# Later requests and later splits of the first second-layer weights in a mixture-of-experts kernel

## The reference

```python
hid  = jax.nn.relu(jnp.einsum('nd,edf->nef', h_flat, exp_w1) + exp_b1)   # D = 256 -> FF = 1024
eout = jnp.einsum('nef,efd->ned', hid, exp_w2) + exp_b2                  # FF = 1024 -> D = 256
y    = jnp.einsum('ned,ne->nd', eout, combine)                           # two experts a row
x    = x + y.reshape(x.shape)
...
df    = -gradv_Af + gradvv_Bf * 0.5
f_new = f + df * dt[:, None, None]
return jnp.maximum(f_new, 0.0)
```

## Time and profile before

| | |
|---|---|
| three executions | 357.04 us median (356.84, 357.04, 358.08) |
| the profiled execution's own time | 358.11 us |
| its span | 356.3 us |
| TensorE busy | 304.0 us, 85% of the span |
| VectorE busy | 285.2 us, 80% |
| ScalarE busy | 252.6 us, 71% |
| GpSimd busy | 160.7 us, 45% |
| DMA moved | 74.27 MB, mean 208 GB/s |

### The profile page before, as it was taken

One profiled execution on the slowest core, in us unless ns is written; L12 is line 12 of the kernel. 1 busy time (PEld: TensorE's weight loads), 2 busy tenths in 40 slices (PEclk: granted clock), 3 DMA queues, 4 the chain that ended last, 5 costly groups with the idle time before them and its releaser, 6 DMA issues.

```text
span 356.3 us, 6562 instructions
## 1 busy us (share of the span) xinstructions
PE 304.0 (85%) x1963; PEld 264.1 (74%) x1963; DVE 285.2 (80%) x523; ACT 252.6 (71%) x465; POOL 160.7 (45%) x136
## 2 busy tenths in 40 slices
PE   1759133899999999999999999999999988467886
PEld 0648123899999999999999999999999978122334
DVE  4896773598899889988888988998898893299991
ACT  1688213796997899699699979969978870188421
POOL 2566306144345445543533554554354413287650
PEclk9999655899999999999999999999999999699999
DMA  7904355886677787766867886776784500596832
GB/s 270 379 7 127 110 225 168 312 265 218 213 256 264 269 278 254 263 198 244 281 205 261 266 294 208 247 242 224 229 266 152 158 3 30 171 300 118 179 103 77
DMA packets 49860, 74.27 MB, mean 208 GB/s; under 512 B 3349, under 2 KB 40751, under 8 KB 49712
## 3 DMA queue, kind: packets, MB, share of 16 engines
q1 hardware_dynamic: 45104, 62.29, 53.5%
q0 software_dynamic: 4368, 11.54, 10.6%
q10 hardware_dynamic: 368, 0.20, 0.2%
HBM read 63.51 MB, written 9.31 MB: 204 GB/s over the span
## 4 chain that ended last, share of the span: by engine, by line
PE 72%; DVE 13%; DMA 6%; ACT 3%; issue 3%; POOL 1%; SPq 1%; DVEq 0%; POOLq 0%; ACTq 0%
PE psum L1005 24%; PE psum L1032 19%; PE psum L1034 10%; PE psum L998 5%; PE psum L974 2%; PE psum L1000 2%; PE psum L1027 2%; DMA t_y<-y_rows 2%; PE psum L1069 1%; DMA x_sb<-t_y 1%; PE psum L913 1%; PE psum L924 1%; DMA x_sb<-in_x_dram 1%; PE psum L1068 1%; DVE t_d1b2f L1540 1%
## 5 line engine op out<-in xcount | busy, mean ns | idle before, releaser
L798 POOL DMA_INDIRECT gathered<-h_rows,src_cur x40 | 64.9, 1622 | 123.1 <-DVE src_cur L1336 103.3
L1032 PE MATMUL psum<-w_split,hid 128*128 128x512 f32 x296 | 106.7, 403 | 1.4 <-DVE y_sb L1388 1.4
L1005 PE MATMUL psum<-slot_h,w_split 128*128 128x256 f32 x768 | 97.4, 287 | 2.3 <-DVE slot_h L1353 1.5
L1005 PEld LDWEIGHTS psum<-slot_h,w_split 128*128 128x128 f32 x768 | 95.4, 195 | 3.5 <-issue 2.9
L1034 PE MATMUL psum<-w_split,hid 128*128 128x256 f32 x296 | 82.8, 280 | 0.0
L1347 DVE TENSOR_TENSOR w_split<-raw_b,w_split 128x2048 fp32r<-128x2048 f32 x23 | 52.7, 2292 | 19.6 <-ACT w_split L622 19.6
L1032 PEld LDWEIGHTS psum<-w_split,hid 128*128 128x128 f32 x296 | 55.6, 188 | 14.1 <-issue 1.7
L654 ACT ACTIVATE hid<-relu 128x512 fp32r<-128x512 f32 (+1 forms) x92 | 51.0, 590 | 16.4 <-DVE relu L1359 16.4
L811 POOL DMA_INDIRECT y_rows<-y_sb,dst_cur x39 | 48.7, 1249 | 28.6 <-issue 11.6
L645 ACT ACTIVATE relu<-psum,b_cur 128x256 f32<-128x256 f32 x128 | 53.6, 490 | 10.8 <-PE psum L1005 9.0
L1341 DVE TENSOR_TENSOR w_split<-raw_a,w_split 128x2048 fp32r<-128x2048 f32 x23 | 52.6, 2285 | 8.8 <-DMA gathered<-h_rows,src_cur 5.9
(11 more groups left out here) (184 smaller groups left out, 395.3 us busy)
## 6 DMA issues: line engine op xcount, KB each, us to landing
raw_a<-in_L_cond_exp_w_dram SPq DMA_DIRECT2D x23, 1024.0 KB, 6.2
raw_b<-in_L_cond_exp_w_dram SPq DMA_DIRECT2D x23, 1024.0 KB, 5.6
t_y<-y_rows SPq DMA_DIRECT2D x6, 512.0 KB, 8.4
x_sb<-in_x_dram SPq DMA_DIRECT2D x4, 512.0 KB, 6.7
h_rows<-h_tok SPq DMA_DIRECT2D x16, 128.0 KB, 2.2
x_sb<-t_y POOLq DMA_DIRECT2D x4, 512.0 KB, 4.8
out_dram<-t_out SPq DMA_DIRECT2D x3, 512.0 KB, 3.0
b_all<-in_L_cond_exp_b_dram SPq DMA_DIRECT2D x1, 1024.0 KB, 10.4
```

Of the source, the lines that this page charges most:

```text
L798: pool.indirect_dma_start(out=gathered[:, par, t, :], out_offset=None, in_=h_rows, in_offset=bass.IndirectOffsetOnAxis(ap=src_cur[:, par, ...
L1005: last = pe.matmul(banks[bank][:, ST * (blk % 2):ST * (blk % 2) + rows], w_split[:, 0, par, w, at:at + P], slot_h[:, par, h, k, 0:rows], s ...
L1032: pe.matmul(out.rearrange("p (w d) -> p w d", w=2), hid[:, par, 0, blk, P * t:P * t + P], w_split[:, 1, par, :, D * blk:D * blk + D], star ...
```

## The change

The wait in front of the load of the second weights of slots 0 and 1 is now for slot 1's rows, where it was for slot 0's. On ACT, the high part of slot 0's second weights is made behind the fourth bank's relus, where it stood behind the first bank's high part, ahead of the high part of slot 1's rows. On DVE its low part is made behind the low part of the second bank, where it stood ahead of it.

```diff
-            sp.wait_ge(rows_in[0], moved(0, None))
+            sp.wait_ge(rows_in[1], moved(1, None))
             for s in range(2):
                 sp.dma_start(w2_raw[s].rearrange("p (b d) -> p b d", b=FB),
...
                 relus(k, m, 1)
                 high(k, m, 0)
                 if k == 0:
-                    split_w2(0, None)
                     split_h(1, None)
                 relus(k, m, 2)
                 high(k, m, 1)
                 relus(k, m, 3)
+                if k == 0:
+                    split_w2(0, None)
                 if k > 0 and not last_slot:
                     split_h(k + 1, m)
...
                     if k == 0:
                         low_h(1, None)
+                    low_hid(k, m, 1)
+                    if k == 0:
                         low_w2(0, None)
-                    low_hid(k, m, 1)
```

## The result

The changed kernel took 360.23 us in the median (359.06 to 360.94, 7 executions), the kernel before 358.08 us (356.84 to 358.42, 7 executions, the three of the prediction among them). The ratio is 1.0066 with a 95% interval of 1.0047 to 1.0085: slower by about 2.1 to 2.4 us, where no change that can be measured was forecast (+0.2 us, with 358.6 as the range's upper end). On the 357.04 us that the forecast started from, the ratio makes 359.4, outside the range as well. The profiled execution took 360.23 us, with a span of 358.4; the one of before had 358.11 and 356.3.

The account below looks back on a forecast made before the run. TensorE was taken to bound the kernel, with 1.14 us of waits to win and ACT and DVE close behind. The -0.76 us gain is given back in a new wait of about 1.0, leaving +0.2: median 357.3 us, range 356.3 to 358.6.

Parts of the forecast that it names:

- the chain through ACT and DVE: Through slot 0's finish to layer 2 of slot 1: ends at 85.20 before, 0.76 us ahead of TensorE; 86.17 after.
- the new wait: TensorE ahead of layer 2 of slot 1, released by DVE's finish of slot 0: about 1.0 us, giving back the -0.76.
- the load of slot 2's first weights: SP's third 1 MB load: lands at 73.2 instead of 69.46; ACT waits 0.4 us and is 0.97 us later than before.
- the upper bound: Slot 2's first weights land as much later as their group starts, 4.6 us, at 74.1.
- a lower bound with 422 GB/s for the third MB: Slot 2's first weights: two loads alone took 7.66 us, a third MB adds 2.5, landing at 72.25.
- the slots behind move with TensorE's +0.2: Behind slot 3's rows, ACT and DVE have idle time to fall back on, so later slots shift by only +0.2 us.
- executions with an early clock: TensorE's clock rises earlier in the ramp: the change loses up to 0.8 us more, +0.2 becoming +1.0.
- all cases with the load or the clock dearer: Rival, chance 0.25: load lands at 74.1 (+0.9) or clock rises early (+0.8), 357.7 to 358.6; both, +1.9 or 358.9.
- TensorE did not keep its gain: Rival, chance 0.16: TensorE keeps its gain at layer 2 of slot 1, up to -1.08 us, 356.0 to 356.6.
- The rows did come earlier: Rival, chance 0.05: slot 1's rows do not come earlier, SP's wait ends at 65.9; +4.9 us, 362.
- The clock did not fall: Rival, chance 0.02: TensorE's clock falls back in the new wait, products at half speed, 359 to 360.
- the signs of being wrong: TensorE has no new wait before layer 2 of slot 1, or ACT's split stands behind its DMA past 74.5.

Follow-up runs that it names:

- e3: Changed kernel, with SP's loads reordered: slot 0's second weights, slot 2's first weights, slot 1's second weights; ratio to the kernel before 1.0002.
- e5: e3, with DVE's finish of slot 0 put ahead of the low part of slot 1's second weights; 357.34 on 357.44 us, 0.9994.
- a1: Changed kernel, no edit, profiled again, clock nearly late; layer 2 of slot 1 starts 27.56 us after slot 0's first product.
- a2: Changed kernel, no edit, profiled again, early clock; layer 2 of slot 1 starts 27.31 us after slot 0's first product.
- e1: Kernel before, with only SP's wait moved to slot 1's rows and ACT's and DVE's order kept; 360.45 on 357.65 us, 1.0076.
- e4: Changed kernel, with slot 3's first weights asked for behind slot 2's second weights; ratio to the kernel before 1.0059.
- e6: Changed kernel, with DVE's index for slot 2's gather made behind the low part of slot 1's rows, so the gather issues later; 360.8 us, 1.0098.
- b1: Kernel before, no edit, profiled again, late clock; layer 2 of slot 1 starts 25.73 us after slot 0's first product.
- b2: Kernel before, no edit, profiled again, early clock; layer 2 of slot 1 starts 24.98 us after slot 0's first product.
- e2: Changed kernel, with SP's wait put back to slot 0's rows, only ACT's and DVE's order moved; 358.98 on 357.65 us, 1.0025.
- e7: Kernel before, with ACT's high part of slot 1's rows ahead of the split of slot 0's second weights; ratio 0.9998.
- e8: e7 plus e5's early finish; SP loads slot 0's second weights, then behind slot 1's rows slot 2's first and slot 1's second; 0.9997.

## Why the prediction was wrong

**What came as forecast.** Slot 1's rows land at 61.95 (62.1 was said), and their transposes follow the first half without a wait. Layer 1 of slot 1 follows at once. The moved split starts at 69.65 (69.88), its DMA in time. Layer 2 of slot 0 starts at 75.23 (75.4). ACT is ready for the split of slot 2's first weights at 72.7 (72.82). From there the chain through ACT and DVE to the finish of slot 0 and to layer 2 of slot 1 is the one named, and the new wait ends on L1389. e3 and e5 confirm its two ends: with the load in time the loss is gone, with the finish moved that wait is gone.

**The step that failed** is "the load of slot 2's first weights". The mechanism was right, the term was too small. I took 73.2 for its landing, the middle between 72.25 and 74.1; it was 74.44. ACT's wait was 1.83 us instead of 0.4, and its start 2.28 us later than before instead of 0.97. In distances from slot 0's first product the split comes 1.48 us later than was said (14.55 against 73.2 - 60.13 = 13.07), and layer 2 of slot 1 1.43 later than the +0.2: this one term is that part of the miss. The grounds for going below the upper bound were that slot 1's gathers no longer share the way, and a lower bound with 422 GB/s for the third MB. The group of three took 12.4 to 12.8 us in the six profiles in which it starts with slot 1's rows (after, a1, a2, e1, e4, e6), more than the 11.8 to 12.1 in the five with slot 1's gathers beside it (before, b1, b2, e2, e7). The nearest row was the group's own, and the upper bound made from it was itself 0.3 us too early.

The estimate by the Trainium skill, DMA: Bandwidth & Descriptors, section "Anatomy of one DMA" (71.3), was 3.1 us too early. The section gives its fit for DMAs issued by GpSimd, and these loads are issued by SP; the prediction did not say so. By the prediction's own sum a load in time would also have lowered the result by 0.4 us (ACT at 72.82 instead of 73.2), not by 0.2.

**The second miss** is in the sum's end: "the slots behind move with TensorE's +0.2", because ACT and DVE had idle time to fall back on. I checked slot 3's rows and stopped there (and took 91.85 for the start of layer 1 of slot 3, which by the timeline is 91.69). DVE did not catch up: it was 2.24 us late at the finish of slot 0 and 2.23 at the low part of slot 4's rows. There the kernel before had less room. From the low part's end to TensorE's start took 0.26 us after (102.29 to 102.55), so its room was 100.70 - 0.26 - 100.06 = 0.38 us, against 0.77 at layer 2 of slot 1 (85.96 - 0.14 - 85.05). The difference of 0.39 is the 0.38 lost there, and the forecast's own 0.97 us of delay would have cost it too. From layer 2 of slot 1 to slot 6 it is 29.9 to 30.0 us in before, b1, b2, e1 and e7, and 30.4 to 30.6 in all the others, e3 with its load in time among them; in e1, where DVE is as late but TensorE later still, nothing is lost.

**The third** is weight. That executions with an early clock lose up to 0.8 us more by the change was said, and b2 and a2 show it: 24.98 to 27.31 is +2.3 at layer 2 of slot 1, against +1.6 with the late clock. With the 0.45 behind it, the loss at slot 6 is 2.76 and 2.07, and the measured 1.0066, 2.4 us, lies between them. But I gave all cases with the load or the clock dearer 0.25, and put both at full size at +1.9, where the profiles show 2.3. In all six profiles that have the group as the change makes it the load was later even than the upper bound of 74.1 (13.97 as a distance; ACT's split, which waits for it, starts at 14.26 to 14.64).

**The rivals.** TensorE did not keep its gain (layer 2 of slot 1, +1.63). The rows did come earlier (61.95). The clock did not fall in the new wait of 1.72 us; it did in e1's of 3.02 us. Of the signs of being wrong that the prediction named, one came, barely: the split stands behind its DMA past 74.5 (74.52).

## What to carry to other kernels

When a wait in a queue is moved, price every transfer behind it by the latest start its consumer can bear, and take for a group's landing the time that the same group took in the same order, not a sum of better parts. Then order the group by who needs what first: here the swap of two loads was worth the whole 2.1 us. And where a chain is made later, look for the place behind it with the least room, not only for the next one: the 0.38 us of room at slot 4 cost 0.4 us more than the 0.77 at slot 1. A wait seen in one profile can be a matter of that execution's clock; where a step hangs on a wait under 1 us near a change of the clock, look at a second profile first, and add up the waits on both sides of it: here one shrank by 0.55 us as the other grew by as much.

## What the runs showed of the hardware that was not expected

- After TensorE had stood still for about 2.2 of 3.02 us its clock went to 1.2 GHz. It stayed there from 70.9 to between 77.5 and 77.9, some 6.8 us, of which it worked for the last 6.0 (e1, the windows above and this one):

```profile
77.90:79.00 1.10, 1.10 (x12) 1.10 (x10) 1.10 (x1) 1.10 (x4) 1.10 (x1) 1.00 1.09 370
```

  Waits of 1.33 (e7) and 1.72 us (after) left it at 2.4 GHz. Two of e1's seven executions took 362.8 and 363.1 us and the others 359.6 to 361.4. Only the one of 363.1 was profiled, and its granted clock over the whole execution is the lowest (0.938). The one of 362.8 has 0.948, as have three of the faster ones, so that the clock explains it too is not shown.
- A group of three loads of 1 MB took 12.4 to 12.8 us from the first issue to the last landing in the six profiles in which it started some 4.5 us later, beside more work of ACT and DVE and with slot 2's gather, and 11.8 to 12.1 in the five with the old start and slot 1's gathers. What makes the 0.4 us and more was not found, but the windows narrow it (the last two columns are the DMA engines' share and GB/s). After, e6 and e4:

```profile
69.00:70.00 1.00, 1.00 (x10) 1.00 (x10) 0.56 (x1) 1.00 (x3) 0.00 (x0) 1.00 1.07 376
70.00:71.00 1.00, 1.00 (x11) 1.00 (x10) 0.00 (x0) 1.00 (x1) 0.00 (x0) 1.00 1.05 177
71.00:72.00 1.00, 1.00 (x11) 1.00 (x10) 0.41 (x1) 1.00 (x3) 0.00 (x0) 1.00 0.96 387
```

```profile
70.00:71.00 1.00, 1.00 (x11) 1.00 (x10) 0.00 (x0) 1.00 (x1) 0.00 (x0) 1.00 1.08 402
```

```profile
73.00:74.00 1.00, 1.00 (x11) 1.00 (x10) 1.00 (x1) 0.37 (x2) 0.00 (x0) 1.00 0.19 78
```

  With the gather at 65.12 the rate falls to 177 GB/s for about a microsecond near 70.5; with the gather at 68.84 (e6) it does not. But by the third landing the plain DMAs of e6 had moved 3.99 MB since the first issue, 0.84 more than the three loads' 3.15, which is slot 3's load; in after it was 0.59 more. In e4, with nothing queued behind, 3.15 MB were moved, and the last 1.7 us before the landing ran at 78 GB/s and less, at a fifth of the engines' share. So e4 and e6 each take one thing away and leave the other in place, and no run takes away both.
- The last stage's reading of the scattered rows, right behind the slots, took 4.3 us in b1 and 7.4 in b2 of the same kernel:

```profile
306.13 4.29 DMA t_y<-y_rows
```

```profile
306.68 7.40 DMA t_y<-y_rows
```

b2's reading ends 3.7 us later than b1's, and its span is 2.3 us longer (357.7 and 355.4), although its slots were 0.8 us faster. Gains under 0.5 us in the slots, as in e5 and e8, were not told beside such differences.
